# Mixture of experts: gates multiplied into the hidden activations, second product channel-major and summed over all experts in PSUM

## The reference

```
def _moe(tokens, router_w, w1, b1, w2, b2):        # tokens: layer norm of t, without weights
    logits = tokens @ router_w.T
    probs = softmax(logits);  rw, re = top_k(probs, 2);  rw = rw / max(rw.sum(-1), 1e-12)
    combine = zeros((N, E)).at[arange(N)[:, None], re].set(rw)
    out = tokens
    for e in range(8):
        h = gelu(tokens @ w1[e] + b1[e])
        y = h @ w2[e] + b2[e]
        out = out + combine[:, e:e + 1] * y
    return out
t = t + _moe(_ln_t(t), ...);  x = _from_tokens(t, x)     # stored as 128 channels x 1024 positions
```

## Time and profile before

| | |
|---|---|
| Median of 3 runs | 1079.38 us (1071.13 to 1083.23) |
| The profiled execution's own time | 1075.48 us |
| Its span | 1073.4 us |
| Busy in the span | PE 894.7 us (83%), PEld 698.4 us, DVE 725.0 us (68%), ACT 523.5 us (49%), POOL 237.7 us (22%) |
| Mean granted TensorE clock | 0.927 of full speed |
| DMA | 36.12 MB, mean 34 GB/s |
| Chain that ended last | PE 48%, DVE 30%, ACT 10%, issue 8%, POOL 2% |

### The profile page before, as it was taken

How to read it: one execution, slowest core, us unless ns; L and a number is a source line. 1 busy time by engine, 2 the same in 40 slices (tenths; PEclk the granted TensorE clock), 3 DMA queues, 4 the chain that set the end, 5 groups by cost and what they waited for, 6 DMA issues and landing times.

```text
span 1073.4 us, 19631 instructions
## 1 busy us (share of the span) xinstructions
PE 894.7 (83%) x7534; PEld 698.4 (65%) x7534; DVE 725.0 (68%) x1959; ACT 523.5 (49%) x795; POOL 237.7 (22%) x250
## 2 busy tenths in 40 slices
PE   3798899889986687887969797878779999999898
PEld 2565655565655565766757575757567878788787
DVE  2857767776663847465665738485777788887875
ACT  1534544455564472645445453645216555565553
POOL 0044011101101324142424233233631100111000
PEclk8889999999987788898989888999989999999999
DMA  5530000000003030303030200205000000000000
GB/s 153 161 118 20 20 11 11 20 20 20 1 0 68 1 69 1 69 1 69 1 69 2 64 5 15 56 8 121 2 1 1 21 20 1 21 20 21 21 1 40
DMA packets 30891, 36.12 MB, mean 34 GB/s; under 512 B 4560, under 2 KB 24912, under 8 KB 30800
## 3 DMA queue, kind: packets, MB, share of 16 engines
q1 hardware_dynamic: 28112, 26.49, 9.9%
q10 hardware_dynamic: 2688, 8.39, 2.9%
HBM read 21.50 MB, written 4.98 MB: 25 GB/s over the span
## 4 chain that ended last, share of the span: by engine, by line
PE 48%; DVE 30%; ACT 10%; issue 8%; POOL 2%; ACTq 2%; SPq 0%; DMA 0%; DVEq 0%; POOLq 0%
DVE cacc L1652 6%; PE ps L997 6%; PE ps L674 6%; DVE acc L1927 3%; PE ps L661 3%; DVE nmax L1509 3%; PE ps L919 2%; PE ps L753 2%; PE ps L628 2%; PE ps L755 2%; PE ps L754 2%; ACT un L1322 2%; ACTq L1242 2%; PE ps L633 2%; PE ps L826 2%
## 5 line engine op out<-in xcount | busy, mean ns | idle before, releaser
L1927 DVE SCALAR_TENSOR_TENSOR acc<-ps,comb,acc 128x128 f32<-128x128 f32 x512 | 141.2, 343 | 22.4 <-PE ps L997 21.8
L997 PEld LDWEIGHTS ps<-w_f,hid 128*128 128x128 f32 x1024 | 131.2, 191 | 16.7 <-ACT hid L1341 8.4
L997 PE MATMUL ps<-w_f,hid 128*128 128x128 f32 x1024 | 136.8, 276 | 4.9 <-ACT hid L1341 4.9
L1341 ACT ACTIVATE hid<-ps,b_f 128x512 f32<-128x512 f32 x128 | 86.2, 685 | 107.7 <-PE ps L755 107.6
L1284 ACT ACTIVATE dcy<-ps 128x1024 f32<-128x1024 f32 x64 | 65.3, 1021 | 91.5 <-PE ps L870 91.4
L1802 DVE TENSOR_TENSOR y_w<-ps,zs 128x256 f32<-128x256 f32 x64 | 27.1, 423 | 120.4 <-PE ps L910 119.9
L1509 DVE TENSOR_REDUCE nmax<-ps 128x1 f32<-128x1024 f32 x64 | 78.1, 1221 | 39.6 <-PE ps L633 39.2
L544 POOL TENSOR_TENSOR srs<-sve,neg_half 128x1 f32<-128x1 f32 x64 | 39.0, 610 | 269.2 <-DVE gram L1761 269.2
L1652 DVE SCALAR_TENSOR_TENSOR cacc<-ps,cw,cacc 128x1023 f32<-128x1023 f32 (+5 forms) x72 | 91.2, 1273 | 4.8 <-ACT cacc L1218 4.2
L1134 ACT ACTIVATE probs<-ps,nmax 128x1024 f32<-128x1024 f32 x64 | 71.3, 1113 | 41.1 <-DVE nmax L1509 38.3
L1744 DVE SCALAR_TENSOR_TENSOR dcy<-dcy,g_sb 128x1024 f32<-128x1024 f32 x64 | 84.1, 1314 | 9.6 <-ACT dcy L1284 8.9
(11 more groups left out here) (211 smaller groups left out, 1910.4 us busy)
## 6 DMA issues: line engine op xcount, KB each, us to landing
c_dec<-exp_dram SPq DMA_DIRECT2D x32, 256.0 KB, 6.2
xc<-in_x SPq DMA_DIRECT2D x8, 512.0 KB, 3.5
q_b<-q_a SPq DMA_DIRECT2D x16, 256.0 KB, 2.8
X<-in_x_tok ACTq DMA_DIRECT2D x8, 512.0 KB, 5.0
c_rep<-cacc ACTq DMA_DIRECT2D x32, 128.0 KB
out<-o_ch SPq DMA_DIRECT2D x8, 512.0 KB, 2.6
w_f<-in_w SPq DMA_DIRECT2D x2, 512.0 KB, 3.6
cst_f<-in_sel_rows SPq DMA_DIRECT2D x1, 512.0 KB, 4.6
```

Of the source, the lines that this page charges most:

```text
L997: last = nc.tensor.matmul(ps[:, Y_BANKS[n], t * P:(t + 1) * P], hid[n % 2][:, t * P:(t + 1) * P], w2_f[:, e, :], start=True, stop=True)
L1341: nc.scalar.activation(hid[n % 2][:], ps[:, 4 + n % 2, :], ACT.Gelu, bias=b1_f[:, n // 2:n // 2 + 1]).then_inc(e_hidden_ready, 1)
L1927: done = nc.vector.scalar_tensor_tensor(acc[u][:, tt, :], ps[:, bank, t * P:(t + 1) * P], comb[u][:, tt, e:e + 1], acc[u][:, tt, :], ALU.m ...
```

## The change

The gates are turned to lie as rows (expert and token block on 64 partitions), written to DRAM, and read back spread over all 128 partitions, one tile of 128 x 1024 for each expert. DVE multiplies `hid` by that tile into `h_gated`. The second product then has `w2` as the stationary and `h_gated` as the moving operand, 512 tokens wide, so that its result is channel-major, and all eight experts accumulate in two PSUM banks for each picture. The sum is started in these banks by `place_sum`: `b2` times the gate rows, and `acc` times the identity. ACT copies the sum straight to the output tile. The scalings by DVE, `turn_out`, `second_biases`, `biases` and the splits of `b2` and of the gates are gone; the order of the threaded parts is another one, and the statistics are computed two pictures ahead.

```diff
 @block.sync
+            def spread_gates(b, u):
+                sp.wait_ge(e_gates_copied, b + 1)
+                sp.dma_start(gates_dram[u], comb_t[:]).then_inc(e_gates_written, 16)
+                sp.wait_ge(e_gates_written, 16 * (b + 1))
+                if b >= 2:
+                    sp.wait_ge(e_gated, 2 * NE * (b - 1))
+                    sp.wait_ge(e_sum_placed, b - 1)
+                if b == 1:
+                    sp.wait_ge(m_out_added, NT * B)
+                for e in range(NE):
+                    if b == 0 and e == 4:
+                        sp.wait_ge(m_out_added, NT * B)
+                    row = gates_dram[u, e * NT:(e + 1) * NT].rearrange("(o t) p -> o (t p)", o=1)
+                    sp.dma_start(gates_b[u][e][:], row.to_broadcast([P, N])).then_inc(e_gates_loaded[e], 16)
+                    if e == 0:
+                        sp.dma_start(gate_rows[u][:], gates_dram[u].rearrange("(e t) p -> e (t p)", t=NT)).then_inc(e_rows_loaded, 16)
+            # SP's order: spread_gates(0); then for each b: store(b - 1), spread_gates(b + 1)
 @block.gpsimd, experts(b)
-                    norm(b + 1, 1 - u)
-                    start_sum(b + 1, 1 - u)
+                if first: norm(1, 1)
+                if not last: start_sum(b + 1, 1 - u)
+                if b + 2 < B: norm(b + 2, u)
 @block.tensor
-            def second(b, n, first):        # four products of hid blocks by w2_f, then e_added on DVE
+            def second(b, n):
+                pe.wait_ge(e_gated, 2 * NE * b + n + 1)
+                nc.tensor.matmul(ps[:, sum_bank(b, h), :], w2_f[:, e, :], h_gated[n % 2][:], start=False,
+                                 stop=(e == NE - 1), skip_group_check=True).then_inc(e_second_product, 1)
-            def second_biases(b): ...
-            def turn_out(b, u): ...
+            def place_sum(b, u):
+                (waits: e_out_ready b - 1 for b >= 2, m_out_added for b == 1)
+                pe.wait_ge(e_rows_loaded, 16 * (b + 1))
+                for h in range(2):
+                    nc.tensor.matmul(ps[:, sum_bank(b, h), :], b2_f[:], gate_rows[u][:, h * BANK:(h + 1) * BANK],
+                                     start=True, stop=False, skip_group_check=True)
+                pe.wait_ge(e_sum_started, b + 1)
+                for t in range(NT):
+                    last = nc.tensor.matmul(cols(ps[:, sum_bank(b, 0):sum_bank(b, 0) + 2, :], t, P), acc[u][:, t, :], id_f[:],
+                                            start=False, stop=False, skip_group_check=True)
             def experts(b, u, first, last):
                 for n in range(2 * NE):
-                    second(b, n, first)
                     (expert n + 2, or of the next picture)
-                    if n == 1 and not first: turn_out(b - 1, 1 - u)
+                    second(b, n)
-                    5: turn_tokens, 7: logits, 12: turn_weights, 13: second_biases
+                    1: turn_tokens, 3: logits, 8: turn_weights, 13: place_sum
+            # before the first picture: expert(0, 0, 0), expert(0, 0, 1), place_sum(0, 0)
 @block.scalar, experts(b)
+                if not last: token_norm(b + 1)            # before gelu(b, 2)
-                    3: store, 5: token_norm, 7: token_high, 9: gate_exponentials
+                    2: store, 3: token_high, 6: gate_exponentials
                 gelu waits for e_gated (n - 2) instead of e_second_product
 @block.vector
-                    # four scalar_tensor_tensor per half expert: acc = ps * comb + acc
+                    dve.wait_ge(e_hidden_ready, 2 * NE * b + n + 1)
+                    if h == 0: dve.wait_ge(e_gates_loaded[e], 16 * (b + 1)); dve.sem_inc(wait_carrier, 1)
+                    if n >= 2 or b > 0: dve.wait_ge(e_second_product, 2 * NE * b + n - 1)
+                    nc.vector.tensor_tensor(h_gated[n % 2][:], hid[n % 2][:], gates_b[u][e][:, h * BANK:(h + 1) * BANK],
+                                            ALU.mult).then_inc(e_gated, 1)
-                    0: statistics, 5: low, 7: largest, 8: places, 10: softmax, 11: weights, 12: turned, 13: biases
+                    2: low, 4: largest, 5: places, 6: softmax, 7: weights, 8: turned, 12: statistics(b + 2)
-                    split_weights: cast and subtraction of b2_blocks; weights: comb_h, comb_s
+                    in the last scan picture, statistics(1) stands where biases(0) stood
```

More of the change, by code:

```diff
@@ L19, in hybrid_kernel @@
                   tri, ones, sel_rows, head_rows,
[L20 removed]
+                  router, w1, b1, w2, b2, iota8, out):
     B, C, N = x.shape
@@ L225, in hybrid_kernel @@
         oh2 = esb("oh2", [P, NT, NE])
[L226 to L229, removed]
+        comb = esb("comb", [P, NE, NT])
+        comb_t = esb("comb_t", [NE * NT, P])
+        gate_rows = [esb("gate_rows0", [NE, N])]
+        gates_b = [[esb(f"gates0_{e}", [P, N]) for e in range(4)]]
         acc.append(esb("acc1", [P, NT, P]))
@@ L463, in _, with experts @@
                 sp.sem_inc(out_free, 1)
+            def experts(b, u, first, last):
+                if not first:
+                    store(b - 1)
+                if not last:
+                    spread_gates(b + 1, 1 - u)
+            spread_gates(0, 0)
+            scanned(sp, experts)
+            store(B - 1)
         @block.gpsimd
@@ L1112, in _ @@
             expert(0, 0, 1)
+            place_sum(0, 0)
             scanned(pe, experts)
-            turn_out(B - 1, 1)
         @block.scalar
@@ L1781, in scan @@
                 if last:
-                    statistics, low, largest, places, softmax, weights, turned, biases = scores(0, 0)
+                    statistics, low, largest, places, softmax, weights, turned = scores(0, 0)
                     parts = [(statistics, (), 1.5), (split_weights, (), 3.5), (low, (), 3.5), (largest, (), 4.5),
                              (places, (), 4.5), (softmax, (), 5.5), (weights, (), 5.5), (turned, (), 6.5),
-                             (biases, (), 7.5)]
+                             (scores(1, 1)[0], (), 7.5)]
                 for c in range(NT):
@@ L1912, in scores @@
[L1912 to L1932 removed]
+                    if b > 0:
+                        dve.wait_ge(e_gates_written, 16 * b)
@@ new lines, in turned @@
+                    nc.vector.tensor_copy(comb_t[:], ps[0:NE * NT, 0, P:2 * P]).then_inc(e_gates_copied, 1)
+                return statistics, low, largest, places, softmax, weights, turned
+            def experts(b, u, first, last):
+                parts = dict(zip((2, 4, 5, 6, 7, 8), scores(b + 1, 1 - u)[1:])) if not last else {}
+                if b + 2 < B:
+                    parts[12] = scores(b + 2, u)[0]
+                for n in range(2 * NE):
+                    e, h = n // 2, n % 2
+                    dve.wait_ge(e_hidden_ready, 2 * NE * b + n + 1)
+                    if h == 0:
+                        dve.wait_ge(e_gates_loaded[e], 16 * (b + 1))
+                        dve.sem_inc(wait_carrier, 1)
+                    if n >= 2 or b > 0:
+                        dve.wait_ge(e_second_product, 2 * NE * b + n - 1)
+                    nc.vector.tensor_tensor(h_gated[n % 2][:], hid[n % 2][:], gates_b[u][e][:, h * BANK:(h + 1) * BANK],
+                                            ALU.mult).then_inc(e_gated, 1)
+                    if n in parts:
+                        parts[n]()
@@ L2014 @@
     none = np.zeros((32, 1024), np.float32)
-    b2_blocks = np.zeros((8, 8, 8, 128), np.float32)
-    for t in range(8):
-        b2_blocks[t, :, t] = g["L1_ffn_b2"]
-    b2_blocks = np.tile(b2_blocks.reshape(64, 1024), (2, 1))
     a |= {
```

173 lines of the change are left out of this document (69 added, 104 removed).

## The result

| | before | after |
|---|---|---|
| Median | 1076.7 us (1071.13 to 1083.23) | 1097.8 us (1088.23 to 1101.78) |
| Ratio, 95% interval | 1 | 1.0168 [1.0123, 1.0214] |
| Span of the profiled execution | 1073.4 us | 1094.0 us |
| Busy in the span | PE 894.7, DVE 725.0 us | PE 917.7, DVE 665.3 us |
| DMA | 36.12 MB | 69.58 MB |

A forecast was written before the change was run, and what follows sets the result against it. PE was taken to bound the expert stage, DVE close behind. 7 x 2.2 = 15.4, +2.4, -1, -4.4 and -2.5 summed to +10 us, giving 1089, lowered to 1087 for downward doubt; range 1070 to 1101 us.

The forecast's parts named there:

- PE's work after: TensorE's work in a picture: 31.4 us, 1.3 more than before, from dearer b2 and acc products; bounds -1.7 to +1.7.
- The waits after: PE's waits in a picture, mostly for DVE's parts in front of second products: 4.3 us against 3.4 before.
- the walk: One picture followed through the engines' queues in time order with trace durations: 35.7 us a picture, 2.2 more.
- The port: DVE's gated product, two SBUF inputs, held beside POOL's addition for up to 2.4 us in n = 2, costing little.
- Start, end, scan: Outside the repeated pictures: first place_sum +2.4 us, first picture -1, end -4.4, last scan picture -2.5 (-3.6 to +0.8).
- The clock: TensorE's granted clock in the expert stage: full at 2.4 GHz, none to be won; no term for losing it.
- the sum, +10: Total over the kernel: seven pictures at 2.2 us more, plus start, end and scan, make it 10 us slower.
- Waits absorbed: Rival, chance 0.12: PE's new order absorbs DVE's parts, 31.9 us a picture, sum -17, 1062 us.
- Gate rows late: Rival, chance 0.13: gate rows reach place_sum 1.8 us late, PE waits 13 us more in all, 1100 us.
- Port bites: Rival, chance 0.12: POOL's root holds a gated product 1.6 us, PE loses 1 us more a picture, 1094 us.
- Nothing moves: Rival, chance 0.08: PE's waits stay at 3.4 us, a picture costs 1.3 us more, 1080 us.
- DVE's 8 us a picture: Saving on DVE in each picture from replacing four scalings (1.13 us) by one gated product (0.62 of the engine).

The follow-up runs named there:

- run 5: Changed kernel with its threaded parts moved to other half experts and the b2 product zero-padded to 128 rows: 1062.78 us, ratio 0.9880 to the kernel before.
- run 4: Changed kernel with only the places of the threaded parts moved, on DVE, PE, ACT and POOL: 1065.37 us, ratio 0.9892 to the kernel before.
- run 3: Changed kernel with PE's order turned back, second product ahead of the next hidden product: 1129.65 us, ratio 1.0462 to the kernel before.
- run 10: Kernel before, with the gates' transposition, b2 products and DVE's last two parts one half expert later: 1067.86 us, ratio 0.9917.
- run 11: Kernel before, with the gates' parts and the rest of the front one half expert later, ACT's parts left in place: 1103.72 us, ratio 1.0251.
- run 12: Kernel before, with the whole front one half expert later, including ACT's token_high and gate exponentials: 1080.92 us, ratio 1.0016.
- run 6: Changed kernel with only DVE's parts, turn_weights and place_sum moved, POOL's start_sum and ACT's store left: 1068.30 us, ratio 0.9899 to the kernel before.
- run 2: Changed kernel with POOL's start_sum held back until DVE's gated product of half expert 5: 1103.82 us, ratio 1.0249 to the kernel before.
- run 7: Changed kernel with the b2 product over 128 rows and ACT's store behind gelu 5 instead of gelu 2: one run, 1084.82 us.
- run 1: Changed kernel with b2 and gate rows zero-padded from 8 to 128 partitions in the b2 product: 1085.78 us, ratio 1.0083 to the kernel before.
- run 8: Changed kernel with the b2 product over 128 rows and gate tiles loaded only an eighth as large from the third picture on: one run, 1084.81 us.

## Why the prediction was right, and what it missed

**PE's work after: 0.3 short.** A half expert takes 1.55 to 1.56. `place_sum` was put at 3.5; with 128 rows it is 3.49 (in run 5 5.05 us from the product n = 15 to the next picture's first, less 1.56), with the 8 rows 3.9 (run 4). The sentence that failed is "The gate rows use 8 partitions, but the time goes by columns": the change of the row count costs 0.2 at the entry and 0.2 at the exit. By the distances, work is 31.7 us after against 29.9 before, so that the new form is 1.8 dearer on PE, where the prediction had 1.3.

**The waits after: right in place, 0.4 too long.** Each of the places named is there. The waits are 3.9 us against 4.3 forecast, and that the picture came out at 35.7 to the tenth is luck: work 0.3 short and waits 0.4 long cancel. Waits before are 3.5 (3.4 forecast). Runs 3 and 4 confirm the walk for other orders (40.4 at full clock against 39.9; 32.3 against 31.9 to 32.5); for the old form it was right once (run 10) and missed twice (runs 11 and 12). That they are DVE's is what the trace names (14.1 of 15.7 us), and run 6 bears it out: moving only DVE's and PE's parts gave everything back. DVE's parts alone weren't moved.

**The port: right.** The product takes 2.25 us beside POOL's addition of 2.37, once a picture; the earlier trace rows had 3.37 for a subtraction twice as wide. The cost is hidden behind the wait for `low`: none by run 2, none by run 6. The Trainium skill's rule (SBUF — State Buffer, "Who interferes with whom"), that the loser blocks fully, nearly agrees: the product ends 0.55 us after the addition (929.87 against 929.32), where alone it takes 0.69.

**Start, end, scan.** Last picture 24.25 (24.2). Scan -3.0 (-2.5). The start lost 4.1 instead of 2.4, since the half clock from 804.8 lay over the hidden products, whose records there stand 0.43 apart instead of 0.23. In run 7, where no half clock lay over it, the start took 5.8 us, against 5.6 forecast.

**The clock: missed.** From "TensorE has its full clock" in the earlier trace rows the prediction concluded that no clock was to be won, and asked no more; that the change could lose it was no term and no rival. This is the term that was put at nothing. In the profiled run it cost 5.1 us in the pictures and about 1.7 at the start. With the chance 4.1 us of the scan this is about the distance between the sum, +10, and the profile, +20.6. Run 1, with neither half clock in the pictures nor the 0.4 us a picture of the loads, has a ratio of 1.0083, +9 us, where the sum had +10.

**The rivals.** Waits absorbed: no, they are 3.9. Gate rows late: no, although its 1100 is nearer to the measured time than the forecast's 1087. PE doesn't wait for `gate_rows`: the copy of the gates ends (906.9) 8.3 us ahead of the `place_sum` at 915.2. Of a picture's eight tiles the first, on which this rival hung, lands 3.8 to 4.4 us after its issue, near the 3.6 of a plain load; the last, issued behind the others, takes 7.0 to 9.9. Port bites: no. Nothing moves: no.

**Where the gain of the new form went.** Of DVE's 8 us a picture little was on the path: PE waits three times in a picture of before, and only once for DVE (1.54 us idle, for the gates); run 10 took most of that away with DVE's work unchanged. On PE the form is dearer by 1.8 us a picture. What decided either way are the places of the threaded parts: 3.4 us a picture in the new form (run 4), 1.1 in the old one (run 10).

**Open.** What makes the clock fall is not shown. It is told here only by its neighbours: 8-row products (2 of 35 places), a wait of 1.5 us ahead of 16-column products (six of six pictures in run 2, and once more behind 0.72 us), a wait of 2 us for a gelu (6 of 7 in run 11). Nor was a form tried in which POOL's addition is gone altogether.

## What to carry to other kernels

When a change moves an engine from behind the bottleneck to in front of it, write its queue down in order of time: a walk with durations from the trace gave each wait of after to within 0.4 us and found a better order. It is no proof for the next order: two of three moves in the old form came out otherwise. Try the same respacing on the old form before crediting the new one. When a part is moved, move what stands for it in every queue, and look at what it used to cover; and ask in the sum what the granted clock could lose, also where the kernel before has it in full.

## What the runs showed of the hardware

- The clock can fall while the records of PE show no gap: 0.50 from 917.4 to 920.8, in after. It doesn't do so each time: the same place is followed by full clock in five of the seven pictures.
- One idle time of 1.47 us in front of sixteen products of 16 columns was followed by 6.8 us of half clock in six of six pictures (run 2); 0.72 us was followed by it in run 2 and in after, and not in run 1. With 1.21 us one half expert earlier and no idle time there, the clock stayed whole in six of six (after).
- Going from 128 to 8 rows in both operands costs 0.2 us, and going back another 0.2: the load of weights comes 0.76 us after the last there, 0.24 with 128 rows.
- A float32 product 512 wide costs 0.87 us (1.56 less 3 x 0.23), four of 128 columns 0.89: the wider tile brings nothing.
- A tile of 512 KB spread from 4 KB in DRAM lands in 3.8 to 4.4 us when it is the first of eight, in 7.0 to 9.9 when it is the last; a plain load of 512 KB in 3.6. Cutting six pictures' tiles to an eighth left the distance at 35.3 (run 8).
